# Scores from 96 stacked rows by way of memory, V split on GpSimd, and routing written with other operations

## What is computed

```python
# attention on the layer-normalised x; keys and values from ctx; 16 heads of width 16
q = split(jnp.einsum('btc,oc->bto', query, wq) + bq) * SCALE     # SCALE = 16 ** -0.5
k = split(jnp.einsum('btc,oc->bto', key, wk) + bk)
v = split(jnp.einsum('btc,oc->bto', value, wv) + bv)
# one block of 128 tokens a sequence: the band mask is causal
attn = jax.nn.softmax(jnp.where(valid, scores, neg_inf), axis=-1)
x = x + jnp.tanh(g_xattn[0]) * (attention output @ wo.T + bo)
# mixture of experts: E = 8, K = 2, cap = 640 rows an expert
xn = (xf - mu) / jnp.sqrt(var + 1e-05) * ln_gamma + ln_beta
top_p, top_i = jax.lax.top_k(softmax(xn @ Wr.T), K)
kept = rank < cap                       # rank: how many earlier slots chose this expert
buf = zeros((E, cap, D)).at[e_s, pos].set(xn[t_s], mode='drop')
h = silu(buf @ W12[:F].T) * (buf @ W12[F:].T);  y = h @ W3.T
out = zeros((T, D)).at[t_s].add(y_slot * weight);  x = x + tanh(g_ffn[0]) * out
```

## Time and profile before

| | |
|---|---|
| median of 3 runs | 535.51 us (535.21 to 535.95) |
| the profiled execution | 534.19 us |
| its span in the trace | 532.3 us |
| part one, until the first product of the experts | about 237 us |
| TensorE busy, share of the span | 479.7 us, 90% |
| VectorE busy | 360.8 us, 68% |
| ScalarE busy | 298.9 us, 56% |
| GpSimd busy | 208.9 us, 39% |
| mean granted TensorE clock | 0.973 of full speed |
| moved by transfers | 57.33 MB |

### The profile page before, as it was taken

How to read it: one execution, slowest core, us unless ns; L and a number is a source line. 1 busy time by engine, 2 the same in 40 slices (tenths; PEclk the granted TensorE clock), 3 DMA queues, 4 the chain that set the end, 5 groups by cost and what they waited for, 6 DMA issues and landing times.

```text
span 532.3 us, 10749 instructions
## 1 busy us (share of the span) xinstructions
PE 479.7 (90%) x3551; PEld 444.7 (84%) x3551; DVE 360.8 (68%) x854; ACT 298.9 (56%) x757; POOL 208.9 (39%) x272
## 2 busy tenths in 40 slices
PE   5699999899999877369998999999999999999991
PEld 4588887777877666269998999999999999999991
DVE  6867888988888997547876574485843768544240
ACT  3689878677778764416664564373723747423230
POOL 8636776787787566510212012203032030311202
PEclk9999999999999997779999999999999999999996
DMA  8868432314142611153677362347451474201111
GB/s 269 209 140 250 78 41 72 75 57 81 42 80 55 205 42 53 58 175 118 234 184 219 78 226 34 60 129 193 132 144 20 130 188 131 31 4 17 13 19 20
DMA packets 41649, 57.33 MB, mean 108 GB/s; under 512 B 3721, under 2 KB 38576, under 8 KB 39552
## 3 DMA queue, kind: packets, MB, share of 16 engines
q1 hardware_dynamic: 35168, 48.62, 31.7%
q0 software_dynamic: 6144, 8.07, 9.1%
q10 hardware_dynamic: 288, 0.00, 0.0%
HBM read 36.24 MB, written 16.72 MB: 99 GB/s over the span
## 4 chain that ended last, share of the span: by engine, by line
PE 55%; DVE 3%; issue 2%; POOL 1%; DMA 0%; ACT 0%; POOLq 0%; DVEq 0%
PE bank L1438 17%; PE bank L1440 17%; PE bank L1439 17%; PE bank L1432 2%; PE bank L1361 1%; PE bank L1304 1%; POOL expert_rows L484 0%; DMA expert_rows<-xr,slotu 0%; DVE pT L929 0%; PE bank L1290 0%; POOL out_tokens L546 0%; DVE nm L924 0%; PE bank L1231 0%; PE bank L1238 0%; DVE osum L938 0%
## 5 line engine op out<-in xcount | busy, mean ns | idle before, releaser
L546 POOL DMA_INDIRECT out_tokens<-ysc,rows x32 | 49.6, 1550 | 245.6 <-DVE ysc L1142 238.9
L1438 PE MATMUL bank<-bXh,wh 128*128 128x384 f32 (+1 forms) x384 | 122.1, 318 | 2.9 <-issue 2.6
L1440 PE MATMUL bank<-bXh,wl 128*128 128x384 f32 (+1 forms) x384 | 121.8, 317 | 0.0
L1439 PE MATMUL bank<-bXl,wh 128*128 128x384 f32 (+1 forms) x384 | 121.8, 317 | 0.0
L749 ACT ACTIVATE sil<-bank 128x384 f32<-128x384 f32 (+1 forms) x96 | 43.7, 456 | 128.4 <-PE bank L1440 127.2
L1121 DVE TENSOR_TENSOR hF<-sil,bank 128x384 f32<-128x384 f32 (+1 forms) x96 | 48.9, 510 | 77.9 <-ACT sil L749 71.3
L633 ACT ACTIVATE p<-bank,nm 128x128 f32<-128x128 f32 x256 | 73.6, 387 | 14.7 <-DVE nm L924 14.7
L1438 PEld LDWEIGHTS bank<-bXh,wh 128*128 128x128 f32 x384 | 72.7, 189 | 3.3 <-issue 3.3
L1438 PE MATMUL bank<-wh,hH 128*128 128x256 f32 x256 | 73.8, 288 | 0.3 <-DVE ysc L1142 0.3
L1439 PEld LDWEIGHTS bank<-bXl,wh 128*128 128x128 f32 x384 | 72.7, 189 | 0.0
L1440 PEld LDWEIGHTS bank<-bXh,wl 128*128 128x128 f32 x384 | 72.6, 189 | 0.0
(11 more groups left out here) (146 smaller groups left out, 878.8 us busy)
## 6 DMA issues: line engine op xcount, KB each, us to landing
stage<-in_w12T SPq DMA_DIRECT2D x16, 1024.0 KB
stage<-in_w3T SPq DMA_DIRECT2D x8, 1024.0 KB
expert_rows<-padrow SPq DMA_DIRECT2D x8, 662.5 KB, 7.9
rows<-expert_rows SPq DMA_DIRECT2D x7, 662.5 KB, 4.4
kM<-k SPq DMA_DIRECT2D x64, 64.0 KB, 2.4
cT<-in_ctxT SPq DMA_DIRECT2D x8, 256.0 KB, 3.1
out_tokens<-x_all SPq DMA_DIRECT2D x8, 256.0 KB, 2.3
x_all<-in_x SPq DMA_DIRECT2D x2, 640.0 KB, 8.5
```

The costliest lines, as they stand in the source:

```text
L546: pool.indirect_dma_start(out=out, out_offset=bass.IndirectOffsetOnAxis(rows[par][:, c, D + E:ROW].bitcast(U32), 0), in_=ysc[par][:, c, :] ...
L1438: nc.tensor.matmul(out_ap, ah, bh, start=start, stop=False)
L1439: nc.tensor.matmul(out_ap, ah, bl, start=False, stop=False)
L1440: return nc.tensor.matmul(out_ap, al, bh, start=False, stop=stop)
```

## The change

What it does, engine by engine:

- **Scores.** From super-block 1 on, keys and queries are laid out so that the 96 rows of a product are high, low and high halves of a pair of heads (`SR = 32` rows each): `qS` holds high, high, low of the queries, `kS` high, low, high of the keys, with the keys of the two heads in separate columns and zeros between. One product of 96 rows and 256 columns then does the three products for two heads; a group has the mask and two such products. The layout is made by SP's `stack`: halves go to DRAM (`qD`, `kD`) and come back by six and three transfers. Super-block 0 keeps the old form (`first_scores`, `spread_first_keys`, one `kM`).
- **Halves.** `kT` and `qT` are gone. ScalarE writes the rounded half straight from PSUM, and VectorE makes the low half from PSUM, bias and high half in one instruction for each 256 columns (`keys_low` at g = 1, `queries_low` at g = 3). The factor 1/4 moves to the input columns.
- **V.** All four steps are on GpSimd, in `values_parts`, at the start of its super-block, right behind the previous `dispatch`.
- **Order.** On TensorE keys, input columns, queries stand at g = 0, 1, 2 (before: columns at 0, keys at 2, queries at 4), behind the weighing and the output's pieces; `ranks` stands at the end of g = 7. ScalarE's order changes with it.
- **Padding** is stored by GpSimd's queue: two blocks ahead of super-block 0, three in 0 and three in 1, then the spare rows. GpSimd also clears `kS[1]`.
- **Routing.** `member` keeps all sequences, and ranks are sums over all earlier ones, with the expert's base in the sum; `seen` and `slot0` are gone; `late` compares with a row of limits; the probability and the gate are one instruction. `orec` lies in PSUM. `bn_aggr` of the second norm waits for GpSimd to have read the value before it.
- The loops of part one are written out.

The diff, cut to its core:

```diff
-        kM = [sb(pa, f"kM{i}", [P, 2, H, SB * T], F32R) for i in range(2)]
+        kM = sb(pa, "kM", [P, 2, H, SB * T], F32R)
+        kS = [sb(pa, f"kS{i}", [P, HP, 2, SB * T], F32R) for i in range(2)]
...
+        orec = [O[i][:, 8 * VW:8 * VW + 8] for i in range(2)]
...
+            def stack_keys(par, part, half):
+
+                for h in range(2):
+                    r = part * SR + h * HD
+                    sp.dma_start(kS[par][r:r + HD, :, h, :].bitcast(F32).rearrange("d (c a) t -> d c a t", c=DC),
+                                 kD[half].rearrange("(a h d) c t -> h d c a t", h=2, d=HD)[h]).then_inc(ld_k, 16)
+
+            def stack_queries(par, part, half):
+
+                sp.dma_start(qS[par][part * SR:(part + 1) * SR, :, :].bitcast(F32).rearrange("r (c a) t -> r c a t", c=DC),
+                             qD[half].rearrange("(a r) c t -> r c a t", r=SR)).then_inc(ld_q, 16)
+
+            def stack(n, par):
+
+                sp.wait_ge(act_kh, DC * (n + 1))
+                sp.dma_start(kD[0], k2[:, 0, :, :].bitcast(F32)).then_inc(sent_kh, 16)
+                sp.wait_ge(dve_kl, n + 1)
+                sp.dma_start(kD[1], k2[:, 1, :, :].bitcast(F32)).then_inc(sent_kl, 16)
+                sp.wait_ge(sent_kh, 16 * n)
+                stack_keys(par, 0, 0)
+                stack_keys(par, 2, 0)
+                sp.wait_ge(sent_kl, 16 * n)
+                stack_keys(par, 1, 1)
+                sp.wait_ge(act_qh, DC * (n + 1))
+                sp.dma_start(qD[0], q2[:, 0, :, :].bitcast(F32)).then_inc(sent_qh, 16)
+                sp.wait_ge(dve_ql, n + 1)
+                sp.dma_start(qD[1], q2[:, 1, :, :].bitcast(F32)).then_inc(sent_ql, 16)
+                sp.wait_ge(sent_qh, 16 * n)
+                stack_queries(par, 0, 0)
+                stack_queries(par, 1, 0)
+                sp.wait_ge(sent_ql, 16 * n)
+                stack_queries(par, 2, 1)
+
+            sp.wait_ge(km_zero, 3)
+            spread_first_keys()
+            sp.wait_ge(ks_zero[1], 1)
+            stack(1, 1)
...
+            def values_parts(n, par):
+
+                v = vf[:, :, :].rearrange(vh, d=HD)
+                pool.wait_ge(act_vf, n + 1)
+                pool.tensor_copy(V3[par][:, :, :, 0:HD], v).then_inc(pool_v, 1)
+                pool.wait_ge(pool_v, 3 * n + 1)
+                pool.tensor_tensor(v, v, V3[par][:, :, :, 0:HD], ALU.subtract).then_inc(pool_v, 1)
+                pool.wait_ge(pool_v, 3 * n + 2)
+                pool.tensor_copy(V3[par][:, :, :, HD:2 * HD], v).then_inc(pool_v, 1)
+                pool.wait_ge(pool_v, 3 * n + 3)
+                pool.tensor_tensor(V3[par][:, :, :, 2 * HD:3 * HD], v, V3[par][:, :, :, HD:2 * HD], ALU.subtract).then_inc(pool_v3, 1)
...
+            values_parts(0, 0)
+            pool.memset(kS[1][:, :, :, :].bitcast(F32), 0.0).then_inc(ks_zero[1], 1)
+            pool.wait_ge(pad_ok, 1)
+            pad((0, 1))
...
             def body(n, par, prev1, prev2, cur, nxt, nxt2, reuse):
+                if cur and prev1:
+                    values_parts(n, par)
+                if nxt2:
+                    normalize_inputs(n + 2)
                 if cur:
-                    values_third(n, par)
                     residual(n, par, prev1)
-                if nxt:
-                    keys_low(n + 1)
+                if n < 2:
+                    pad((3 * n + 2, 3 * n + 3, 3 * n + 4))
+                if n == 1:
+                    zero_spare_rows()
                 if prev1:
                     norm2(n - 1, 0)
                     if cur:
                         normalize2(n - 1, 1 - par, 0, reuse)
-                if nxt2:
-                    normalize_inputs(n + 2)
-                if nxt:
-                    queries_low(n + 1, 1 - par)
                 if prev1:
                     norm2(n - 1, 1)
                     if cur:
                         normalize2(n - 1, 1 - par, 1, reuse)
-                if nxt:
-                    values_rest(n + 1, 1 - par)
...
-            def keys(n, bank, prev1):
+                    act.activation(halves[:, 0, t, :], bank[:, t * SB * T:(t + 1) * SB * T], ACT.Identity, bias=bq4[:, t:t + 1])\
+                       .then_inc(act_qh, 1)
+
+            def keys(n, bank):
                 act.wait_ge(pe_k, n + 1)
-                if prev1:
-                    act.wait_ge(pool_kl, n)
+                if isinstance(n, int) and n == 1:
+                    for half in ld_km:
+                        act.wait_ge(half, KM)
+                elif not isinstance(n, int) or n > 1:
+                    act.wait_ge(sent_kh, 16 * (n - 1))
                 for t in range(DC):
-                    act.activation(kT[:, t, :], bank[:, t * SB * T:(t + 1) * SB * T], ACT.Identity, bias=bqkv[:, 1, t:t + 1])\
-                       .then_inc(act_k32, 1)
-                if prev1:
-                    for half in ld_km:
-                        act.wait_ge(half, KM * n)
-                act.wait_ge(act_k32, DC * (n + 1))
-                act.activation(k2[:, 0, :, :], kT[:, :, :], ACT.Copy).then_inc(act_kT, 1)
+                    act.activation(k2[:, 0, t, :], bank[:, t * SB * T:(t + 1) * SB * T], ACT.Identity, bias=bqkv[:, 1, t:t + 1])\
+                       .then_inc(act_kh, 1)
...
-                dve.wait_ge(dve_r, R_CHAIN * m + 4)
-                dve.tensor_scalar(xr[mpar][:, :, D:D + E], prob[:, :, :], tg[:, 1:2], None, ALU.mult).then_inc(dve_wp, 1)
+                dve.wait_ge(dve_r, R_CHAIN * m + 3)
+                dve.scalar_tensor_tensor(xr[mpar][:, :, D:D + E], lex[:, :, :], tg[:, 1:2], lrc[:, :].unsqueeze(2).to_broadcast([P, SB, E]),
+                                         ALU.mult, ALU.mult).then_inc(dve_wp, 1)
...
-                dve.tensor_scalar(late[:, :, :], rk, float(CAP), LATE, ALU.is_ge, ALU.mult).then_inc(dve_rk, 1)
-                dve.tensor_tensor(slot0[:, :, :], rk, ebase[:, :].unsqueeze(1).to_broadcast([P, SB, E]), ALU.add).then_inc(dve_rk, 1)
-                dve.tensor_reduce(seen_add[:, :], member[:, :, :].rearrange("p j e -> p e j"), AX_X, ALU.add).then_inc(dve_rk, 1)
+                dve.tensor_tensor(late[:, :, :], rk, limit[:, :].unsqueeze(1).to_broadcast([P, SB, E]), ALU.is_ge).then_inc(dve_rk, 1)
                 if probs_between:
                     invert_sum(m)
-                dve.wait_ge(dve_rk, R_SLOT * m + 3)
-                dve.tensor_tensor(slot[:, :, :], slot0[:, :, :], late[:, :, :], ALU.add).then_inc(dve_rk, 1)
-                dve.tensor_tensor(seen[:, :], seen[:, :], seen_add[:, :], ALU.add)
-                if probs_between:
-                    expert_probs(m)
-                dve.wait_ge(dve_rk, R_SLOT * m + 4)
+                dve.wait_ge(dve_rk, R_SLOT * m + 1)
+                dve.scalar_tensor_tensor(slot[:, :, :], late[:, :, :], LATE, rk, ALU.mult, ALU.add).then_inc(dve_rk, 1)
+                dve.wait_ge(dve_rk, R_SLOT * m + 2)
...
+            def keys_low(n, bank):
+                if isinstance(n, int) and n == 1:
+                    for half in ld_km:
+                        dve.wait_ge(half, KM)
+                elif not isinstance(n, int) or n > 1:
+                    dve.wait_ge(sent_kl, 16 * (n - 1))
+                dve.wait_ge(act_kh, DC * (n + 1))
+                for t in range(DC):
+                    ins = dve.scalar_tensor_tensor(k2[:, 1, t, :], bank[:, t * SB * T:(t + 1) * SB * T], bqkv[:, 1, t:t + 1],
+                                                   k2[:, 0, t, :].bitcast(F32), ALU.add, ALU.subtract)
+                ins.then_inc(dve_kl, 1)
...
+            def scores(G, g, n, par):
+                b, hq = g // GPS, g % GPS
+                mask(G, g, False)
+                if g == 0:
+                    pe.wait_ge(ld_k, 6 * 16 * n)
+                    pe.wait_ge(ld_q, 3 * 16 * n)
+                for a in range(2):
+                    ins = nc.tensor.matmul(S[g % 2][:, a * 2 * T:(a + 1) * 2 * T].rearrange("p (h t) -> p h t", h=2),
+                                           qS[par][0:3 * SR, 2 * hq + a, b * T:(b + 1) * T],
+                                           kS[par][0:3 * SR, 2 * hq + a, :, b * T:(b + 1) * T],
+                                           start=False, stop=(a == 1))
                 ins.then_inc(pe_s, 1)
...
+                    elif g == 7 and prev2:
+                        pe.wait_ge(dve_x2, SB * n)
+                        ranks(n - 2, Xo)
+
                     if g == 0 and nxt:
+                        keys(n + 1, 1 - par, Xp, use)
+                    elif g == 1 and nxt:
                         input_columns(n + 1, False, not prev1)
-                    if cur and g >= 3:
-                        weigh_values(G - 3, g - 3, n, par, not prev1 and g < 7)
-                    elif prev1 and g < 3:
-                        weigh_values(G - 3, NG + g - 3, n - 1, 1 - par, False)
-                    if g == 0 and prev1:
-                        if prev3:
-                            pe.wait_ge(dve_rk, 5 * (n - 3) + 2)
```

(10 more changed lines are left out.)

285 lines of the change are left out of this document (134 added, 151 removed).

## The result

The changed kernel takes 556.05 us (median of 4 runs, 554.80 to 557.97); the kernel before, beside it, 535.36 (4 runs). The ratio is 1.038, 95% interval 1.034 to 1.043. The forecast was 536.3 us with a range of 528 to 544: both missed. The profiled execution took 555.65 us with a span of 553.9; before it was 534.19 and 532.3.

| stretch | before, us | after, us | difference | forecast |
|---|---|---|---|---|
| up to the end of V of super-block 3 | 94.26 | 116.36 | +22.1 | -1.7 |
| from there to the end of V of super-block 7 | 96.97 | 94.55 | -2.4 | +4.2 |
| from there to the first product of the experts | 45.45 | 46.97 | +1.5 | -1.6 |
| the experts | 295.6 | 296.0 | +0.4 | 0 |

What follows compares the result with a forecast made beforehand. Attention and routing were taken as bound by a loop between GpSimd's V and VectorE's statistics. +4.2 there, -1.7 at the start and -1.6 at the tail gave +0.9 us on 534.19; forecast 536.3 us, range 528 to 544.

Steps and rivals of the forecast that it cites:

- The start: Up to V of super-block 3: keys and queries through memory start super-block 2 at 59.8 us; -1.7 us at that V.
- VectorE's own 18 us: Super-block 2's start to V of super-block 3: VectorE's work up to the second statistics, 18 of 32.8 us.
- Rival 3: Padding or its issues delay super-blocks 1 and 2 by 5 to 10 us: 541 to 547 us, chance 0.15.
- The ring: Attention and routing: GpSimd writes V, VectorE returns statistics; 25.3 us a super-block against 24.24, +4.2 us over four.
- GpSimd's half: Second statistics to V written, on GpSimd: 12.44 us grows to 14.3, with two V copies of 0.75 us.
- The other half: V written to the next second statistics, through TensorE and VectorE: 11.73 us shrinks to 10.6.
- The clock's 0.4: TensorE's longer waits for V lower its granted clock, costing 0.4 us a super-block, between 0 and 1.5.
- rival 1: Super-blocks of 24.1 us, with copies of 0.55 us and the clock kept: 531.5 us, chance 0.22.
- I cost the scores at nothing on the path: Attention scores: 3.2 us less TensorE work a super-block, but none of it shortens the path.
- VectorE: VectorE's work a super-block: low halves +1.7, L948's blocking -1.9, other savings -0.9; 21.7 us becomes about 20.6.
- Rival 2: V is ready early and VectorE sets 20.6 to 21.5 us a super-block: 521 to 525 us, chance 0.05.
- The tail: Stretch up to the last eight scatters, led by VectorE: fewer instructions and blockings give -1.6 us.

Runs made afterwards that it cites:

- V first: The changed kernel with GpSimd's four steps on V of the next super-block put ahead of the token numbers and four scatters: 547.9 us.
- late padding: The changed kernel with all padding issued by GpSimd at the start of super-block 2 and awaited ahead of the first scatters: 557.7 us.

## Why the prediction was wrong, step by step

- **"The start", the step that failed.** The prediction put the end of stack(1) at 39 us, super-block 2 at 59.8 and V of super-block 3 another 32.8 us behind it; super-blocks 1 and 2 began at 50.5 and 78.8, and V followed 37.6 us later. That is 23.8 us more than forecast, in three places:
  - *Super-block 1, 11.5 us.* The chain began at 26.5 us instead of 22, because two tensor_scalar on VectorE, not costed beside GpSimd's memset, took 6.76 us (with the zeros on GpSimd it began at 21.57). And the sum left the route 17 us, from 22 to 39. That is what it takes without padding (16.2 and 17.1 us measured), so its own length was right; what was left out is the padding, with which it took 24.0. "At the low end it lies in GpSimd's free time" looked at the engine that issues the padding, while its bytes were moved ahead of the query reads.
  - *Super-block 2, another 7.5 us.* The same collision once more, with four further transfers issued from 61.33 us.
  - *From there to V, 4.8 us.* "VectorE's own 18 us" was no path: up to the second statistics it took 23.5 us (22.3 before), with VectorE busy 16.2 of them and TensorE 21.75, at a granted clock of 0.88.

  The place of the padding is shown by experiment: moved behind the reads (and the context loads ahead of it) it gave back 8.7 us, and put off to super-block 2 it took the stop along. Rival 3 named this mechanism, for both routes, with a chance of 0.15 and its condition, stack(1) ending after 42 us, was met (the last reads were issued up to 46.4); but it sized the delay at 5 to 10 us, where it was 11.8 at super-block 1 and 19.5 at super-block 2. TensorE's granted clock of 0.81 to 0.85 from 20 to 60 us (1.00 before) comes on top; no run separates it.
- **The ring.** Forecast 25.3 us, measured 23.64. GpSimd's half was right within 0.4 (copies 0.62 in place of 0.75). The other half was 0.8 shorter. The clock's 0.4 didn't come: 0.93 in the first of the four super-blocks, 1.00 in the others, and all four took 23.62 to 23.66 us, with five waits for V of 2.1 us in the mean and 4.8 at the longest, where six of about 3 were forecast. For this stretch rival 1, the shorter ring, was right (a chance of 0.22; it decides under 24.7 us), and by its own test, 25.3 right and under 24.2 wrong, the forecast's ring was wrong. The Trainium skill, GPSIMD Engine Reference, Engine selection, calls one-input operations "roughly line-rate", which the prediction turned into an estimate of 0.5 us for a copy (512 elements at the page's 1.2 GHz are 0.43, before any fixed cost); the copies of 0.61 to 0.65 us lie between that and the forecast's 0.75.
- **"I cost the scores at nothing on the path"** was wrong with V late, by up to 1.4 us a super-block (11.22 or 11.24 against 9.78 us at the full clock; the new order and routing are in this too), and right with V early. The forecast credited the other half with 1.4 us for the blockings and L862, where the blockings alone gave 0.5 (11.73 to 11.22), and with nothing for the scores: two errors that partly cancel, so that this half came within 0.8 us by luck.
- **VectorE.** L948's counterpart takes 0.29 us throughout, as forecast, the low halves 0.47 each (L956 was the right row). The reciprocals alone gave 0.6 us a super-block where the clock stayed full. VectorE's work was 19.8 us a super-block, where 20.6 was forecast.
- **Rival 2, the ring opens.** Forecast 20.6 to 21.5 us a super-block by VectorE's busy time; with V first it was 23.35. Busy time isn't a period: each group's steps go from engine to engine.
- **The tail.** -1.6 forecast, +1.5 measured. TensorE had stood 4.76 us for V of super-block 7 just before, and from 211 to 220 its granted clock was 0.63 while it was busy 8.96 of 9 us. In the kernel before, the clock was 0.83 from 200 to 220. What the clock cost here was not separated.
- **Padding's issue on GpSimd**: 0.9 us apiece, just under the low end of the bounds; the issues were not what cost time.
- **Routing.** Forecast as a gain for VectorE; alone it made the kernel before 0.5% slower. Of that only the place is shown (the experts' first products), not the cause.

## What to carry to other kernels

When a change sends data through memory, write down per super-block which bytes stand in each queue ahead of the read that the next stage waits for; an average share of the engines says nothing of it, and the same eight pieces of padding gave 547.4, 548.6, 556.1 or 557.7 us by the place where they and the wait for them stood. Let an edit move one transfer and look at what it lets pass: taking the queries off SyncE's queue sent the padding ahead of them. A step on the critical ring that doesn't need what stands before it in its engine's program should be moved ahead: four instructions put ahead of four scatters gave 8 us in one kernel and 17 in the other. Before two turns of a ring are compared, look at their granted clocks: 27.1 and 25.1 us were turns of one program, at 0.89 and 1.00. And when a ring is opened, the next period is not the largest busy time but the latency of the steps that hand over to each other.

## What was not expected of the hardware

- Two tensor_scalar of 128x2048 in a row on VectorE took 1.2 and 5.6 us (from 16.81 and 17.9 us). The first ran beside GpSimd's subtraction, which took 2.21 us in place of 1.15; the second was under way when GpSimd went on to its memset of 3.51 us (18.98 to 22.49), and ended only after it. Three other kernels show the same 5.6 us. In the one with V first they took 1.2 and 2.2 us, and the memset, from 18.64, took 4.59: there GpSimd was the one to wait. With the two engines apart (late padding) they took 1.2 us each. So the same instructions, started 0.3 us apart in two kernels, lost VectorE 4.4 us in one, and VectorE 1.0 and GpSimd's memset 1.1 in the other. What decides between the two was not tested.
- Three reads of 256 KB landed some 4.7 us after their last issue with nothing new behind the key reads (39.6 to 44.3), and 8.6 us after it with four stores of 662.5 KB issued since just before them (37.1 to 45.7).
- The granted clock was 0.63 from 211 to 220 us, behind TensorE's wait of 4.76 us for V, and 0.93 to 1.00 over the four super-blocks with waits of 1 to 2 us; at the start, in the windows with the waits of 5.6 and 7.1 us, it was 0.85 and 0.71. In the kernel with V behind the scatters, two super-blocks of one and the same program ran at 0.88 and 0.89 and took 27.1 us, the next two at 1.00 and took 25.1 and 25.0.
